# Twelve attention steps in another order on every engine, and value weights of 17 columns in 32-column groups

## The chip, the cores and the metric

The kernel runs on one core of a Trainium2 chip. The time is the device time of one execution in microseconds (us); the figure quoted is the median of several executions. TensorE is called PE (its weight loads PEld), VectorE DVE, ScalarE ACT, GpSimd POOL, and SyncE, which only issues DMAs here, SP.

## What is computed

A patch step (a product and a layer norm), one attention block and one mixture-of-experts block over 32 sequences of 188 tokens, 256 wide. The change touches attention alone. The reference, cut to it:

```python
q = x @ W_q; k = x @ W_k; v = x @ W_v
latent_kv = (k + v) @ W_down_kv
k_rec = (latent_kv @ W_up_k)   # 16 heads of 16
v_rec = (latent_kv @ W_up_v)
scores = einsum('bhqd,bhkd->bhqk', qh, k_rec) / sqrt(256)
scores = scores * decay          # exp(-0.01 |i - j|)
attn = softmax(scores)
out = einsum('bhqk,bhkd->bhqd', attn, v_rec) @ W_o
h = h + out
```

## The kernel before

Every engine runs its own program, and semaphores tie them together. Stages follow one another: patch step, attention, shared experts with the choice of tokens, experts. Attention takes one sequence ("batch" b) per turn, and each engine walks through `batch(b, par)` with twelve steps n = 0 to 11 (`NS`). A step handles two of the 24 score tiles of a batch, and what the engines do in a step belongs to different batches, since the stages are pipelined.

On PE a step n is: `take_max` (adds the negated row maximum to score tile n-1 by a product with a selection matrix), `scores` (of a tile 18 steps ahead, only to find row maxima), then in steps 1, 4, 7, 10 `weigh` (attention weights times values for four heads), a `job` that hangs on n, and `turned_scores` (the tile of step n+1, the one that is exponentiated). The jobs before are: n=0 second half of the value product (`project_values(b+1, ., 1)`), n=3 the q product (`project`), n=5 the k product, n=8 the output product (`project_out`), n=9 `turn_max` (three transposes of the row maxima), n=11 the first half of the value product of b+2 and `turn_x` (four transposes of the normed input of b+4).

On DVE a step is `row_max` (two tiles) and `times_decay` (one pair of tiles in PSUM), and further `invert` after n=5, `add_out` after n=9, `row_stats` after n=10, the row moments around n=11, and last `low_max`, which writes the low half of the turned maxima. `turn_x` in step 11 and `take_max` of the next batch wait for `low_max` (semaphore `mt_ready`), because the maxima and the turned input share a PSUM bank.

ACT does `exponential` in each step, brings products out of PSUM (`evacuate`, `keep_heads`, `evacuate_values`), makes high fp16 halves (`high`) and spreads values into the tiles V (`values`). POOL makes the low halves (`low`), sends the weighed heads out (`heads_out`), reads them back in dense form (`dense_heads`) and divides (`divide`). The q product in step 3 waits for `xtl_ready`, the low half of x that POOL makes with `low(XTL, ...)`.

`weigh` before takes 128 rows of V by 64 columns: two heads stand side by side in 32-column groups of their own, with zeros where a row belongs to the other head, and the two halves of PE's columns work on two head pairs.

```python
for t in range(3):
    for u in range(2):
        v = (t * HP + 2 * g + u) * 64
        last = mm(OB[64 * u:64 * u + 64, :], V[cpar][:, v:v + 64], PT[:, p:p + S], start=t == 0, stop=t == 2)
```

A product of float32 operands shows in the trace as two matmul records. The order of the work is written out by hand: the place of each call in `batch` is its place in the engine's queue. Lines in the profile before: L1455 take_max, L1441 scores, L1467 turned_scores, L1483 weigh, L1493 q and k product, L1504 values, L1516 output, L1529 turn_max, L1524 turn_x; L1127 row_max, L1136 times_decay, L1099 add_out, L1105 row_stats, L1112 and L1118 moments, L1083 low_max; L756 all copies of ACT, L805 exponential; L612 low, L618 and L619 heads_out, L628 dense_heads, L635 and L639 divide.

## Time and profile before

| what | value |
|---|---|
| median of 3 executions | 2015.07 us (2008.25 to 2016.47) |
| profiled execution | 2018.32 us, span of its instructions 2016.4 us |
| attention, from its first weighing record to the last | 192.0 to 928.8 us |
| batches in attention | 32 |

The profile shows one execution. The granted clock of PE is 1.0 at 2.4 GHz and 0.5 at 1.2 GHz. "Idle before" of a row is the time that the engine stood still ahead of it, with what ended it. Busy time of PE counts a matmul until its modelled end, so that a busy PE need not be one at its peak: the distance between starts tells what a matmul takes.

### The profile page before, as it was taken

The page shows a single profiled execution, that of the slowest core. Times are in us where ns is not written, and L with a number is a line of the kernel's source. Part 1 is how long each engine was busy: PE and PEld are TensorE (multiplying, and loading weights), DVE is VectorE, ACT ScalarE, POOL GpSimd, SP SyncE. Part 2 cuts the span into 40 slices and gives each one's busy share as a digit, 9 for nine tenths or more (in the row PEclk, how much of TensorE's full clock was granted, in tenths as well). Part 3 has the DMA queues.
Part 4 walks back from the last instruction along what each step waited for, and adds up shares of the span by engine and source line. Part 5 has one row for each costly group of instructions (what it writes and reads, how often), then busy time and mean ns, then how long its engine had stood idle before and what let it go on. Part 6 is the DMA issues. An engine that isn't in the chain of part 4 may idle for free.

```text
span 2016.4 us, 46453 instructions
## 1 busy us (share of the span) xinstructions
PE 1751.3 (87%) x14894; PEld 1327.7 (66%) x14894; DVE 1232.4 (61%) x3822; ACT 934.9 (46%) x2157; POOL 947.8 (47%) x945
## 2 busy tenths in 40 slices
PE   6857887887888878785899995999999999999997
PEld 5855665665666666563677773777777777777775
DVE  3884666666666666674767866555555555555551
ACT  3535555444554545452533254444444444444442
POOL 3852333333332333324622323466666666666665
PEclk9987888889987988898999996999999999999999
DMA  5524444444443434442321104243443344443322
GB/s 179 187 77 88 102 103 98 97 93 93 97 98 88 101 93 98 100 96 68 105 51 32 30 27 159 84 114 98 102 109 94 101 111 97 99 97 98 94 31 29
DMA packets 220234, 187.39 MB, mean 93 GB/s; under 512 B 165624, under 2 KB 200952, under 8 KB 214008
## 3 DMA queue, kind: packets, MB, share of 16 engines
q1 hardware_dynamic: 193272, 141.99, 26.0%
q0 software_dynamic: 26880, 44.36, 11.0%
q8 instruction: 46, 0.75, 0.2%
q14 instruction: 36, 0.29, 0.1%
HBM read 135.37 MB, written 50.44 MB: 92 GB/s over the span
## 4 chain that ended last, share of the span: by engine, by line
PE 70%; DVE 10%; issue 8%; POOL 6%; ACT 3%; DMA 2%; DVEq 1%; SPq 1%; POOLq 0%; ACTq 0%
PE psum L1742 24%; PE psum L1759 12%; PE psum L1483 6%; PE psum L1607 6%; PE psum L1493 4%; PE psum L1627 4%; PE psum L1467 2%; PE psum L1516 2%; PE psum L1455 2%; DVE psum L1136 2%; ACT arena L756 2%; PE psum L1504 2%; PE psum L1441 2%; POOL arena L612 1%; DVE arena L1127 1%
## 5 line engine op out<-in xcount | busy, mean ns | idle before, releaser
L1742 PE MATMUL psum<-arena,hidden 128*128 128x376 f16 x3072 | 493.7, 323 | 1.1 <-DVE arena L1362 0.9
L655 POOL TENSOR_TENSOR arena<-arena 128x376 f16<-128x376 f32 x320 | 319.7, 1001 | 353.7 <-ACT arena L756 352.3
L1742 PEld LDWEIGHTS psum<-arena,hidden 128*128 128x128 f16 x3072 | 301.1, 98 | 189.5 <-issue 1.9
L1136 DVE TENSOR_TENSOR psum<-psum,constants 128x376 f32<-128x376 f32 x384 | 212.9, 555 | 218.7 <-PE psum L1467 218.5
L756 ACT ACTIVATE arena<-arena 128x376 f16<-128x376 f32 (+5 forms) x610 | 283.6, 473 | 58.8 <-DVE arena L1298 46.6
L805 ACT ACTIVATE arena<-psum 128x376 f32<-128x376 f32 x384 | 184.9, 482 | 232.5 <-PE psum L1455 227.0
L971 ACT ACTIVATE arena<-psum 128x376 f32<-128x376 f32 x256 | 123.9, 484 | 342.7 <-PE psum L1742 342.7
L756 ACT ACTIVATE arena<-psum 128x376 f32<-128x376 f32 (+7 forms) x457 | 167.6, 398 | 228.5 <-PE psum L1483 123.5
L1127 DVE CUSTOM_DVE_ANT_0 arena<-psum,constants 128x188 f32<-128x188 f32 x768 | 237.6, 347 | 41.2 <-PE psum L1441 36.0
L1372 DVE SCALAR_TENSOR_TENSOR arena<-psum,arena 128x376 f32<-128x376 f32 x256 | 140.8, 550 | 189.9 <-ACT arena L971 188.5
L1759 PE MATMUL psum<-hidden,arena 128*128 128x256 f16 (+1 forms) x2304 | 256.6, 273 | 0.0
L1759 PEld LDWEIGHTS psum<-hidden,arena 128*128 128x128 f16 (+1 forms) x2304 | 229.8, 103 | 21.8
L1354 DVE SCALAR_TENSOR_TENSOR hidden<-arena,hidden 128x512 f16<-128x512 f32 x192 | 205.6, 1075 | 9.1 <-ACT hidden L756 9.1
L612 POOL TENSOR_TENSOR arena<-arena 128x376 f16<-128x376 f32 x128 | 115.2, 900 | 182.9 <-ACT arena L756 177.6
L701 POOL DMA_INDIRECT out<-hidden,arena x96 | 149.9, 1561 | 45.2 <-DVE hidden L1382 23.1
L1483 PE MATMUL psum<-arena 128*64 128x188 f32 x1536 | 167.6, 358 | 1.8 <-ACT arena L805 1.8
L1493 PE MATMUL psum<-arena,weights_hi 128*128 128x188 f16 x512 | 89.1, 276 | 74.7 <-POOL arena L612 65.0
L1455 PE MATMUL psum<-arena 128*128 128x188 f16 x768 | 135.5, 260 | 18.9 <-DVE psum L1136 18.6
L1382 DVE TENSOR_SCALAR hidden<-psum,arena 128x256 f32<-128x256 f32 x96 | 46.3, 482 | 164.7 <-PE psum L1759 164.5
L1441 PE MATMUL psum<-arena 96*128 96x188 f16 x768 | 136.2, 262 | 3.6 <-DVE arena L1127 2.6
L1607 PE MATMUL psum<-arena,weights_hi 128*128 128x376 f16 x512 | 136.3, 327 | 1.2 <-DVE arena L1165 1.2
L1467 PE MATMUL psum<-arena 96*128 96x188 f16 x768 | 135.1, 260 | 0.1
(158 smaller groups left out, 2801.2 us busy)
## 6 DMA issues: line engine op xcount, KB each, us to landing
arena<-q_halves SPq DMA_DIRECT2D x384, 47.0 KB, 2.1
arena<-k_halves SPq DMA_DIRECT2D x384, 47.0 KB, 2.1
arena<-e_g SPq DMA_DIRECT2D x16, 1024.0 KB
arena<-e_u SPq DMA_DIRECT2D x16, 1024.0 KB, 5.1
arena<-e_d SPq DMA_DIRECT2D x16, 1024.0 KB
arena<-x_t SPq DMA_DIRECT2D x32, 376.0 KB, 3.5
weighed<-arena POOLq DMA_DIRECT2D x32, 376.0 KB, 3.3
q_halves<-arena SPq DMA_DIRECT2D x32, 188.0 KB, 3.1
```

What stands on the lines that cost most here:

```text
L655: nc.gpsimd.tensor_tensor(dst, f, hi, ALU.subtract).then_inc(ready, 1)
L756: return nc.scalar.activation(dst, src, ACT.Copy, scale=scale)
L805: nc.scalar.activation(PT[:, i % 6 * 2 * S:(i % 6 + 1) * 2 * S], TB[i % 3], ACT.Exp).then_inc(exp_done, 1)
L1127: last = nc.vector.tensor_tensor_reduce(out=SC[i % 2 * 2 + u], in0=SB[i % 2][:, u * S:(u + 1) * S], in1=C[:, C_DECAY + t * S:C_DECAY + (t ...
L1136: nc.vector.tensor_tensor(TB[i % 3], TB[i % 3], C[:, at:at + 2 * S], ALU.mult).then_inc(multiplied, 1)
L1354: nc.vector.scalar_tensor_tensor(WEL[par][:, c], WST[:, c], WSCALE, WEH[par][:, c], ALU.mult, ALU.subtract).then_inc(wl_ready[i], 1)
L1441: last = mm(SB[i % 2][:, u * S:(u + 1) * S], block_tile(QD[cpar][0:2 * KR, :], a, t), KX[cpar][0:2 * KR, a * S:(a + 1) * S], start=True, s ...
L1455: last = mm(TB[i % 3][:, u * S:(u + 1) * S], block_tile(SEL, a, t), MT[cpar][:, 0:S], start=False, stop=True, skip_group_check=True)
L1483: last = mm(OB[64 * u:64 * u + 64, :], V[cpar][:, v:v + 64], PT[:, p:p + S], start=t == 0, stop=t == 2)
L1607: last = mm(bank[2 * (m % 2) + i][:, 0:CHUNK], w_, a, start=n == 0, stop=n == 5)
L1742: last = mm(bank[2 * (s % 2) + i][:, 0:CHUNK], w_, a, start=n == 0, stop=n == 5)
L1759: last = mm(bank[down_bank[m]][0:rows, 0:D], a, w_, start=n == 0, stop=n == 23)
```

## The change

1. `weigh` loads 17 value columns (16 and the row-sum column) per head into a 32-column group. Four heads go to the four column groups of PE. Per group of four heads there are four products of 128 rows, and then four of 64 rows (the middle tile, whose upper 64 rows belong to one head of a pair and whose lower ones to the other). Before there were six products of 128 rows and 64 columns. V shrinks from 64 to 32 columns for a pair.
2. The order of work changes in `batch` of all engines. PE: `turn_max` goes from n=9 to n=7, the first half of the values from n=11 to n=9 (and into a place of its own, the upper half of PSUM bank 5). ACT: `keep_heads` goes behind the copies of its step, `high_max` from n=10 to 8, x_norm from 8 to 9, the value copies are spread over n=2 and n=11. DVE: `low_max` from n=11 to 9, `add_out` from 9 to 10, `row_stats` from 10 to 11, the moments into the next batch. POOL: `low(XTL)` comes first, and `divide` goes from the end of a batch to the next one.
3. The columns of W_q and W_k are put in the order (half, d, pair), so that the reads of the dense q and k tiles are two DMAs of whole rows instead of six of 188-element pieces. SP reads KD before it waits for the inverse sums.
4. Two more batches are written out ahead of the loop, and one more behind it.

```diff
-        OB, XB, WB = bank[5][:, 0:S], bank[6], bank[7]
+        OB, VB, XB, WB = bank[5][:, 0:S], bank[5][:, D:2 * D], bank[6], bank[7]
...
-            for b in range(-4, 2):
+            for b in range(-4, 4):
                 body(b, b % 2)
-            with nc.Fori(1, B // 2 - 2, engines=bass.OrderedEngineSet([eng.engine]), head_slot={eng.engine: 0}) as i:
+            with nc.Fori(2, B // 2 - 2, engines=bass.OrderedEngineSet([eng.engine]), head_slot={eng.engine: 0}) as i:
                 body(2 * i, 0)
                 body(2 * i + 1, 1)
-            for b in range(B - 4, B + 2):
+            for b in range(B - 4, B + 3):
...
-            def read(blocks, dense, dram, c, lows, par, landed):
-                for h2 in range(2):
-                    for r in range(3):
-                        p = h2 * KR + r * HD
-                        if blocks is not None:
-                            dst = blocks[par][p:p + HD, :].rearrange("p (a n) -> p a n", n=CW)[:, :, h2 * HS:h2 * HS + S]
-                        else:
-                            dst = dense[par][p:p + HD, :].rearrange("p (a n) -> p a n", n=S)
-                        sp.dma_start(dst, rows(dram, c, h2, lows[r])).then_inc(landed[par], 16)
+            def read(blocks, dense, dram, c, single, par, landed):
+                both = 1 - single // 2
+                if blocks is None:
+                    for low, r, n in ((1, single, 1), (0, both, 2)):
+                        src = dram[c, low, :, :, :].rearrange("h (d a) n -> (h d) (a n)", a=HP)
+                        sp.dma_start(dense[par][32 * r:32 * (r + n), :], src.unsqueeze(0).broadcast_to((n, 32, HP * S)) if n > 1 else src).then_inc(landed[par], 16)
+                else:
+                    for h2 in range(2):
+                        for r in range(3):
+                            p = 32 * r + HD * h2
+                            sp.dma_start(blocks[par][p:p + HD, :].rearrange("p (a n) -> p a n", n=CW)[:, :, h2 * HS:h2 * HS + S],
+                                         dram[c, int(r == single), h2, :, :].rearrange("(d a) n -> d a n", a=HP)).then_inc(landed[par], 16)
...
-                    read(QD, None, q_dram, c, (0, 1, 0), par, s_in)
+                    read(QD, None, q_dram, c, 0, par, s_in)
                     sp.wait_ge(k_out, 16 * c + 16)
                     hold(sp)
-                    read(None, KX, k_dram, c, (0, 0, 1), par, s_in)
+                    read(None, KX, k_dram, c, 2, par, s_in)
                 if valid(b + 1):
                     at_least(sp, st_done, NS * b)
                     hold(sp)
-                    read(None, QX, q_dram, b + 1, (0, 1, 0), 1 - par, st_in)
+                    read(None, QX, q_dram, b + 1, 0, 1 - par, st_in)
+                    read(KD, None, k_dram, b + 1, 2, 1 - par, st_in)
                 c = b - 1
                 if valid(c):
                     sp.wait_ge(sums_inverse, c + 1)
                     hold(sp)
+                    at_least(sp, rd_in, 64 * c)
+                    hold(sp)
                     sp.dma_start(r_dram[:, :].rearrange("h (q n) -> (h q) n", q=4), RS[0:64, :]).then_inc(rs_out, 16)
-                if valid(b + 1):
-                    read(KD, None, k_dram, b + 1, (0, 0, 1), 1 - par, st_in)
...
             def batch(b, par):
+                low(XTL[1 - par], XF, XTH[1 - par], xth_ready, b + 3, xtl_ready)
+                heads_out(b - 1, 1 - par)
+                divide(b - 2)
                 low(OTL, ON, OTH, oth_ready, b - 2, otl_ready)
-                heads_out(b - 1, 1 - par)
-                low(XTL[1 - par], XF, XTH[1 - par], xth_ready, b + 3, xtl_ready)
+                low(QS[:, 2 * S:4 * S], QF, QS[:, 0:2 * S], qh_ready, b + 3, ql_ready)
                 dense_heads(b - 1)
-                low(QS[:, 2 * S:4 * S], QF, QS[:, 0:2 * S], qh_ready, b + 3, ql_ready)
                 low(KS2[:, 2 * S:4 * S], KF, KS2[:, 0:2 * S], kh_ready, b + 3, kl_ready)
-                divide(b - 1)
...
             def batch(b, par):
                 for n in range(NS):
                     exponential(b, par, n)
-                    if n == 1:
-                        keep_heads(b - 1, 1 - par, 3)
-                    elif n % 3 == 1:
-                        keep_heads(b, par, (n - 4) // 3)
                     if n == 0:
                         evacuate(XF, XB, b + 3, xt_done, xf_ready)
                     elif n == 1:
                         if valid(b + 3) and valid(b + 1):
-                            act.wait_ge(v_done, b + 2)
+                            act.wait_ge(v_done, 2 * b + 4)
                         high(XTH[1 - par], XF, b + 3, xf_ready, xth_ready)
-                        evacuate_values(b + 1)
-                    elif n in (2, 3):
-                        values(b + 1, 1 - par, n - 2)
+                        keep_heads(b - 1, 1 - par, 3)
+                    elif n == 2:
+                        evacuate_values(b + 1, 1)
+                        values(b + 1, 1 - par, 0)
+                    elif n == 3:
+                        values(b + 1, 1 - par, 1)
                     elif n == 4:
                         evacuate(QF, WB, b + 3, q_done, qf_ready)
+                        keep_heads(b, par, 0)
                     elif n == 5:
                         high(QS[:, 0:2 * S], QF, b + 3, qf_ready, qh_ready, q_out)
                     elif n == 6:
                         evacuate(KF, WB, b + 3, k_done, kf_ready)
                     elif n == 7:
                         high(KS2[:, 0:2 * S], KF, b + 3, kf_ready, kh_ready, k_out)
+                        keep_heads(b, par, 1)
                     elif n == 8:
+                        high_max(b + 1, 1 - par)
+                    elif n == 9:
                         x_norm(b + 4)
                     elif n == 10:
-                        high_max(b + 1, 1 - par)
+                        keep_heads(b, par, 2)
+                    elif n == 11:
+                        evacuate_values(b + 2, 0)
...
             def batch(b, par):
                 for n in range(NS):
-                    if n == 11:
-                        row_moments(b - 2)
+                    if n == 0:
+                        row_moments(b - 3)
                     row_max(b, par, n)
                     times_decay(b, n)
-                    if n == 5:
+                    if n == 0:
+                        keep_moments(b - 3)
+                    elif n == 5:
                         invert(b - 1)
                     elif n == 9:
+                        low_max(b + 1, 1 - par)
+                    elif n == 10:
                         add_out(b - 2)
-                    elif n == 10:
+                    elif n == 11:
                         row_stats(b - 2, 0)
                         row_stats(b - 2, 1)
-                    elif n == 11:
-                        keep_moments(b - 2)
-                        low_max(b + 1, 1 - par)
...
                 at_least(pe, os_ready, 4 * c + g)
+                if g == 3 and valid(c + 2):
+                    pe.wait_ge(vf_ready, 2 * c + 5)
                 pe.wait_ge(exp_done, NS * c + 3 * g + 3)
-                for t in range(3):
-                    for u in range(2):
-                        v = (t * HP + 2 * g + u) * 64
-                        p = (6 * g + 3 * u + t) % NS * S
-                        last = mm(OB[64 * u:64 * u + 64, :], V[cpar][:, v:v + 64], PT[:, p:p + S], start=t == 0, stop=t == 2)
+                for n in range(2):
+                    for k in range(4):
+                        a, h2 = 2 * g + k // 2, k % 2
+                        t, p0, rows = ((0, 0, 128), (2, 0, 128))[h2] if n == 0 else (1, 64 * h2, 64)
+                        v, p = (t * HP + a) * 32, (3 * a + t) % NS * S
+                        last = mm(OB[32 * k:32 * k + HD + 1, :], V[cpar][p0:p0 + rows, v:v + HD + 1], PT[p0:p0 + rows, p:p + S],
+                                  start=n == 0, stop=n == 1)
                 last.then_inc(weighed, 1)
...
                 if n == 0 and valid(b + 1):
+                    if valid(b - 3):
+                        pe.wait_ge(y_added, b - 2)
+                    else:
+                        pe.wait_ge(kf_ready, b + 3 if valid(b + 2) else B)
                     project_values(b + 1, 1 - par, 1)
                 if n == 3 and valid(b + 3):
                     if valid(b + 1):
-                        pe.wait_ge(vf_ready, b + 2)
+                        pe.wait_ge(vf_ready, 2 * b + 4)
                     else:
                         at_least(pe, kf_ready, b + 3)
                     pe.wait_ge(xtl_ready, b + 4)
...
                 if n == 5 and valid(b + 3):
                     pe.wait_ge(qf_ready, b + 4)
                     project(b + 3, 1 - par, W_K, k_done)
+                if n == 7 and valid(b + 1):
+                    if isinstance(b, int) and b + 1 == 0:
+                        pe.wait_ge(cleared, 3)
+                    if valid(b + 3):
+                        pe.wait_ge(xf_ready, b + 4)
+                    pe.wait_ge(scaled, NS * b + 2 * NS)
+                    turn_max(b + 1, 1 - par)
                 if n == 8 and valid(b - 2):
                     if valid(b + 3):
                         pe.wait_ge(kf_ready, b + 4)
                     elif valid(b + 1):
-                        pe.wait_ge(vf_ready, b + 2)
+                        pe.wait_ge(vf_ready, 2 * b + 4)
                     else:
-                        pe.wait_ge(y_added, b - 2)
+                        at_least(pe, y_added, b - 2)
                     pe.wait_ge(otl_ready, b - 1)
                     project_out(b - 2)
-                if n == 9 and valid(b + 1):
-                    if isinstance(b, int) and b + 1 == 0:
-                        pe.wait_ge(cleared, 2)
-                    if valid(b + 3):
-                        pe.wait_ge(xf_ready, b + 4)
-                    pe.wait_ge(scaled, NS * b + 2 * NS)
-                    turn_max(b + 1, 1 - par)
-                if n == 11 and valid(b + 2):
+                if n == 9 and valid(b + 2):
                     pe.wait_ge(xtl_ready, b + 3)
-                    if valid(b - 2):
-                        pe.wait_ge(y_added, b - 1)
-                    else:
-                        pe.wait_ge(kf_ready, b + 4)
+                    if valid(b + 1):
+                        pe.wait_ge(vf_ready, 2 * b + 4)
+                    if valid(b):
+                        pe.wait_ge(os_ready, 4 * b + 2)
                     project_values(b + 2, par, 0)
...
+    by_pair = np.arange(D).reshape(HP, 2, HD).transpose(1, 2, 0).reshape(D)
```

POOL's order, one batch of the loop before (low halves of the output input, `heads_out`, low half of x, `dense_heads`, low halves of q and k, `divide`):

```order
L612 TENSOR_TENSOR arena<-arena 128x376
L616 ISA
L618 DMA arena<-arena 64x1x47
L619 DMA weighed<-arena 128x4x188
L611 REGISTER_ALU
L612 TENSOR_TENSOR arena<-arena 128x376
L623 ISA
L628 DMA arena<-weighed 128x1x188 x2
L612 TENSOR_TENSOR arena<-arena 128x376 x2
L635 TENSOR_TENSOR arena<-arena 128x376
L639 CAST arena<-arena 128x376
```

The same batch on POOL in the changed kernel, where the first row is the low half of x:

```order
L613 TENSOR_TENSOR arena<-arena 128x376
L617 ISA
L621 DMA arena<-arena 64x1x47
L622 DMA weighed<-arena 128x4x188
L635 ISA
L638 TENSOR_TENSOR arena<-arena 128x376
L642 CAST arena<-arena 128x376
L613 TENSOR_TENSOR arena<-arena 128x376 x2
L626 ISA
L631 DMA arena<-weighed 128x1x188 x2
L613 TENSOR_TENSOR arena<-arena 128x376
```

The low half of x no longer stands behind the two DMAs of `heads_out`, and `divide` (L638, L642) of the batch before stands in the middle.

DVE's order before, from `times_decay` of step 10 on: statistics, moments, step 11, and `low_max` (8x192) at its end:

```order
L1136 TENSOR_TENSOR psum<-psum,constants 128x376
L1105 BN_STATS arena<-hidden 94x6
L1105 ISA
L1105 BN_STATS arena<-hidden 94x6
L1112 BN_AGGR arena<-arena 94x2 x2
L1127 ISA arena<-psum,constants 128x188
L1136 TENSOR_TENSOR psum<-psum,constants 128x376
L1118 COPY mean_var<-arena 94x4
L1083 SCALAR_TENSOR_TENSOR arena<-psum,arena 8x192 x2
```

In the changed kernel, from `times_decay` of step 9 on:

```order
L1143 TENSOR_TENSOR psum<-psum,constants 128x376
L1087 ISA
L1090 SCALAR_TENSOR_TENSOR arena<-psum,arena 8x192 x2
L1130 REGISTER_ALU
L1134 ISA arena<-psum,constants 128x188
L1143 TENSOR_TENSOR psum<-psum,constants 128x376
L1106 ISA
L1106 SCALAR_TENSOR_TENSOR hidden<-psum,hidden 94x512
```

`low_max` now stands behind step 9 and ahead of `add_out` and the statistics.

PE's order before around a weighing (step 4, then the turned scores and the next step):

```order
L1441 MATMUL psum<-arena 128x188 x2
L1476 ISA
L1483 MATMUL psum<-arena 64x188 x6
L1467 MATMUL psum<-arena 128x188 x2
L1455 MATMUL psum<-arena 128x188 x2
```

And in the changed kernel (the first number of a product is its weight columns):

```order
L1450 MATMUL psum<-arena 128x188 x2
L1485 ISA
L1495 MATMUL psum<-arena 17x188 x8
L1476 MATMUL psum<-arena 128x188 x2
L1464 MATMUL psum<-arena 128x188 x2
```

Six products of 64 columns became eight of 17; nothing else around them moved.

## Rows read from the trace of the kernel before

**Rows 1.** The page's busy time, share of the span and instructions of each engine.
```profile
PE 1751.3 (87%) x14894; PEld 1327.7 (66%) x14894; DVE 1232.4 (61%) x3822; ACT 934.9 (46%) x2157; POOL 947.8 (47%) x945
```
**Rows 2.** PE's waits, 150 to 935 us: waiter, releaser: total us, times, longest.
```profile
PE psum L1493 <- POOL arena L612: 65.0, 31, 3.3
PE psum L1524 <- DVE arena L1083: 54.4, 29, 2.7
PE psum L1455 <- DVE psum L1136: 18.6, 80, 0.8
```
**Rows 3.** Line L618 (`heads_out`), 300 to 800 us: first and last start, landing.
```profile
L618 POOL DMA_DIRECT2D arena<-arena x21: 627/627/641, 302.5 to 791.3; - x21
...
DMA to landing us min/median/max: 1.9/2.1/2.5
```
**Rows 4.** Timeline of PE: start, length, line, shapes (weights, moving).
```profile
311.04 1.18 PE L1483 MATMUL psum<-arena 128*64 128x188 f32 x12
312.15 0.34 PE L1467 MATMUL psum<-arena 96*128 96x188 f16 x2
312.32 0.33 PE L1455 MATMUL psum<-arena 128*128 128x188 f16 x2
...
316.98 0.38 PE L1504 MATMUL psum<-weights_hi,arena 128*128 128x256 f16 x2
...
317.31 0.38 PE L1504 MATMUL psum<-weights_hi,arena 128*128 128x256 f16 x2
...
319.65 0.51 PE L1524 MATMUL psum<-constants,arena 94*128 94x94 f32 x4 [1.86 <-DVE arena L1083]
320.00 0.33 PE L1467 MATMUL psum<-arena 96*128 96x188 f16 x2
```
**Rows 5.** Timeline of DVE from step 9 to step 11 of a batch.
```profile
339.59 0.68 DVE L1099 SCALAR_TENSOR_TENSOR hidden<-psum,hidden 94x512 f32 x1
340.19 0.34 DVE L1127 CUSTOM_DVE_ANT_0 arena<-psum,constants 128x188 f32<-128x188 f32 x1
...
340.73 0.55 DVE L1136 TENSOR_TENSOR psum<-psum,constants 128x376 f32<-128x376 f32 x1
341.19 0.74 DVE L1105 BATCH_NORM_STATS2 arena<-hidden 94x6 f32 x2
342.08 0.24 DVE L1112 BATCH_NORM_AGGREGATE arena<-arena 94x2 f32<-94x6 f32 x2
...
343.40 0.16 DVE L1118 COPY mean_var<-arena 94x4 f32 x1
343.59 0.71 DVE L1083 SCALAR_TENSOR_TENSOR arena<-psum,arena 8x192 f16<-8x192 f32 x2
```
**Rows 6.** Timeline of PE: router products in four 32-column groups, then full width.
```profile
970.20 0.34 PE L1638 MATMUL psum<-arena,weights_hi 128*32 128x376 f16 x4
...
971.01 0.33 PE L1638 MATMUL psum<-arena,weights_hi 128*32 128x376 f16 x4
971.28 0.33 PE L1607 MATMUL psum<-arena,weights_hi 128*128 128x376 f16 x1
```
**Rows 7.** Timeline of POOL: `heads_out` and the low half of x.
```profile
325.98 0.63 POOL L618 DMA_DIRECT2D arena<-arena  x1 [4.68 <-ACT arena L756]
...
327.44 0.91 POOL L612 TENSOR_TENSOR arena<-arena 128x376 f16<-128x376 f32 x1
```
**Rows 8.** Timeline of ACT: `keep_heads`, then the high half of x.
```profile
325.03 0.33 ACT L756 ACTIVATE arena<-psum 128x188 f32<-128x188 f32 x1 [1.47 <-PE psum L1483]
325.25 0.51 ACT L756 ACTIVATE arena<-arena 128x376 f16<-128x376 f32 x1
```
**Rows 9.** Windows: us, then busy (count) of PE, PEld, DVE, ACT, POOL; PEclk; DMA share; GB/s.
```profile
50.00:100.00 50.00, 43.77 (x379) 41.91 (x377) 42.86 (x170) 26.23 (x53) 39.64 (x22) 0.97 0.58 188
...
150.00:188.00 38.00, 24.66 (x160) 17.45 (x161) 13.10 (x82) 17.05 (x37) 8.08 (x9) 0.64 0.36 77
...
300.00:400.00 100.00, 80.09 (x725) 61.27 (x724) 66.84 (x291) 52.36 (x142) 32.68 (x43) 0.89 0.42 97
```

More of the change, by code:

```diff
@@ L189, in build @@
         MT = [at2(HS, F16) for _ in range(2)]
-        V = [at2(3 * HP * 64) for _ in range(2)]
+        V = [at2(3 * HP * 32) for _ in range(2)]
         at3 = Place()
@@ L829, in x_norm, with evacuate_values @@
                 last.then_inc(xn_ready, 1)
-            def evacuate_values(c):
+            def evacuate_values(c, t):
                 if valid(c):
-                    act.wait_ge(v_done, c + 1)
-                    copy(VF[:, 0:D], WB[:, 0:D], 1.0 / WSCALE)
-                    copy(VF[0:TAIL, D:2 * D], WB[0:TAIL, D:2 * D], 1.0 / WSCALE).then_inc(vf_ready, 1)
+                    act.wait_ge(v_done, 2 * c + t + 1)
+                    if t == 0:
+                        at_least(act, v_ready, 5 * c)
+                        copy(VF[:, 0:D], VB, 1.0 / WSCALE).then_inc(vf_ready, 1)
+                    else:
+                        copy(VF[0:TAIL, D:2 * D], WB[0:TAIL, D:2 * D], 1.0 / WSCALE).then_inc(vf_ready, 1)
             def values(c, par, h2):
@@ L844, in values @@
                     at_least(act, weighed, 4 * c - 4)
-                to = V[par].rearrange("p (t a h w) -> p t a h w", t=3, a=HP, h=2)[:, :, :, h2, 0:HD]
-                first, second = (VF[:, w * D:(w + 1) * D].rearrange("p (a h d) -> p a h d", h=2, d=HD)[:, :, h2, :] for w in range(2))
-                if h2 == 0:
-                    copy(to[:, 0], first).then_inc(v_ready, 1)
-                    copy(to[0:TAIL, 1], second[0:TAIL]).then_inc(v_ready, 1)
-                else:
-                    copy(to[64:128, 1], first[0:64]).then_inc(v_ready, 1)
-                    copy(to[0:64, 2], first[64:128]).then_inc(v_ready, 1)
-                    copy(to[64:64 + TAIL, 2], second[0:TAIL]).then_inc(v_ready, 1)
+                for t, p0, n, q0, at in (((0, 0, 128, 0, 0), (1, 0, TAIL, 0, D)), ((1, 64, 64, 0, 0), (2, 0, 64, 64, 0), (2, 64, TAIL, 0, D)))[h2]:
+                    src = VF[q0:q0 + n, at:at + D].rearrange("p (a h d) -> p a h d", h=2, d=HD)[:, :, h2, :]
+                    dst = V[par][p0:p0 + n, :].rearrange("p (t a w) -> p t a w", t=3, w=32)[:, t, :, 0:HD]
+                    copy(dst, src).then_inc(v_ready, 1)
             def high_max(c, par):
@@ L1497, in project_values @@
             def project_values(c, par, t):
-                rows = (128, TAIL)[t]
+                rows, to = ((128, VB), (TAIL, WB[0:TAIL, D:2 * D]))[t]
                 n = 0
@@ L1503, in project_values @@
                     for a, w_ in split3(XTH[par][:, x], XTL[par][:, x], WH[:, w], WL[:, w]):
-                        last = mm(WB[0:rows, t * D:(t + 1) * D], a, w_, start=n == 0, stop=n == 5)
+                        last = mm(to, a, w_, start=n == 0, stop=n == 5)
                         n += 1
-                if t == 1:
-                    last.then_inc(v_done, 1)
+                last.then_inc(v_done, 1)
             def project_out(c):
@@ L1534, in job @@
                 if n == 0 and valid(b + 1):
+                    if valid(b - 3):
+                        pe.wait_ge(y_added, b - 2)
+                    else:
+                        pe.wait_ge(kf_ready, b + 3 if valid(b + 2) else B)
                     project_values(b + 1, 1 - par, 1)
@@ L1795, in score_tables @@
     select = (p[:, None, None] % 32 == np.arange(HP)[None, :, None]) & (p[:, None, None] // 32 % 2 == row // HS) & inside
-    value_rows = np.zeros((128, 3, HP, 2, 32), np.float32)
-    for h2 in range(2):
-        value_rows[:, :, :, h2, HD] = (inside & (row // HS == h2)).reshape(3, 128).T[:, :, None]
+    value_rows = np.zeros((128, 3, HP, 32), np.float32)
+    value_rows[:, :, :, HD] = inside.reshape(3, 128).T[:, :, None]
     return {"select": (16.0 * select).astype(np.float16).reshape(128, HP * CW), "blank": np.zeros((128, HP * CW), np.float16),
-            "value_rows": value_rows.reshape(128, 3 * HP * 64)}
+            "value_rows": value_rows.reshape(128, 3 * HP * 32)}
 def kernel(x, L0_tok_conv_w, L0_tok_conv_b, L0_tok_ln_gamma, L0_tok_ln_beta, L0_attn_W_q, L0_attn_W_k, L0_attn_W_v,
```

17 lines of the change are left out of this document (9 added, 8 removed).

## The prediction

> **What bounds the kernel now.** The page comes first: PE is the busiest engine at 87% of the span and nothing else passes 61% [rows 1], so the question is where PE stands still inside the changed stage. The table of PE's waits over attention answers it [rows 2]. Two rows carry nearly all: the q product waits for POOL's low half of x, 65.0 us in 31 waits, which is 2.1 us per batch; and `turn_x` waits for DVE's `low_max`, 54.4 us in 29 waits, 1.9 us per batch. A third row, `take_max` waiting for `times_decay`, is 18.6 us or 0.6 us per batch; that is the lockstep between PE and DVE. The length of a batch comes from one POOL line that occurs once in each: 21 starts from 302.5 to 791.3 us are 20 batches of 24.44 us [rows 3]. Last the windows: in a steady stretch of 100 us PE is busy 80.09 us at a granted clock of 0.89 [rows 9], so that about 22% of the time runs at the lower level of 1.2 GHz.
>
> Both waits have a cause that the timelines show. POOL waits 4.68 us for ACT before the first DMA of `heads_out`, issues for 1.46 us (325.98 to 327.44), and only then makes the low half of x in 0.91 us [rows 7], although ACT had finished the high half at 325.76 [rows 8]. DVE comes to `low_max` at 343.59, behind `add_out`, the statistics, the moments and the two steps 10 and 11 [rows 5].
>
> **The change, part by part.** The account is per batch, in the profiled execution (2018.32 us), 24.44 us before.
>
> *The wait for the low half of x.* In the new order POOL makes it first. Counted from PE's start s of step 1: `take_max` takes 0.17 us (312.15 to 312.32 for such a pair) [rows 4], the exponential some 0.5 us and the high half 0.51 us [rows 8], with 0.2 us of latency that is s + 1.3; POOL's 0.91 us [rows 7] make it s + 2.25. PE meanwhile has step 1 (three pairs and a weighing, 1.4 us), step 2 (0.5 us) and two pairs of step 3 (0.34 us), so it asks at s + 2.25. I take the 2.1 us as gone; a rest of 0 to 0.3 us is in the range. `keep_heads` now follows the high half, which delays `heads_out` to about s + 2.3. Its sums land 0.63 + 2.1 us after the issue begins at the latest [rows 3, 7], that is s + 5.0, and DVE wants them after step 5, at about s + 5.9. This cover is thin: 0.9 us.
>
> *The wait for `low_max`.* `turn_max` at step 7 is asked for only after `row_max` of step 6, which `take_max` of step 7 has waited for anyway. `low_max` then stands behind step 9 on DVE, and `turn_x` behind weighing and two steps of PE later. The 1.9 us go as a wait for this row. ACT's copy of q now stands ahead of `keep_heads`, which helps step 5, and a copy of values stands behind the exponential of step 2, which may hurt step 3; I let the two cancel.
>
> *The weighing.* Now 1.11 us from its first start to the next line's (311.04 to 312.15) for 12 records in two halves of the columns [rows 4]. Six pairs at 188 columns and two cycles per column are 6 x 0.157 = 0.94 us, and 0.17 us go before the full width resumes. The nearest row for four column groups is the router product: 24 matmuls in six rounds of four, the sixth round 0.81 us after the first, 0.162 us per round, and 0.27 us from the last round to the next line [rows 6]. Each of its matmuls is as long as a record here (376 columns at one cycle). Eight products are 16 records or four rounds: 4 x 0.157 + 0.17 = 0.80 us, plus something where the second four products, of 64 rows, begin. The rows show 0.10 us more at a change of width than inside one (0.27 against 0.17) and I take 0.05 to 0.1, so 0.85 us, a gain of 0.26 us each and 1.04 us per batch. The bounds: 0.31 us each if the change of rows costs nothing, and no gain if the 64-row products with different rows follow one another (four rounds for them instead of two, 0.31 us more).
>
> The Trainium skill ("TensorEngine Tiling (Array Packing)", Key Properties) says that changing the tiling mode drains the engine, and by that each group now pays one drain more, between 128-row and 64-row tiles. No row here shows that one. By the difference seen at a change of width it is the 0.1 us already in the sum; were it as large as the 0.27 us of the router, a weighing would gain 0.1 us instead of 0.26, and the sum below would be 20.4 us per batch and 1892 us.
>
> *What takes their place.* With both waits gone DVE becomes the partner that PE waits for. A DVE step is 0.54 us of `row_max` (340.19 to 340.73) and 0.46 us of `times_decay` (340.73 to 341.19), 1.00 us [rows 5]. From step 9 to step 0 it does four such steps, `low_max` 0.71, `add_out` 0.60, statistics 0.89, moments 0.24 and 0.16: 6.6 us. PE does in its steps 9, 10, 11 and 0: four times three pairs (2.0), two halves of the value product at 0.66 (316.98 to 317.31 is three of six), one weighing (0.9 with its entry) and `turn_x` 0.35: 4.6 us [rows 4, 5]. PE therefore comes about 2.0 us too early, less some 0.3 us that DVE is ahead after PE's long step 8, so 1.7 us, in steps 0 and 1. The short steps 2 and 6 (0.5 us on PE) cost 0.3 us each as they do now. Sum of waits for DVE: 2.3 us against the present 0.6, 1.7 us more. Everything else DVE, ACT and POOL do is the same work in another place. SP issues 16 reads per batch instead of 24; PE waits for none of them in [rows 2], so they count as nothing. The written-out batches and the extra one at the end are 1 us at most.
>
> *The clock.* At 0.89 about 5.4 us of each batch run at 1.2 GHz, and with PE busy four fifths of it that loses 2.15 us. Of the windows, PE 88% busy has 0.97 (50 to 100 us), 80% has 0.89, 65% has 0.64 [rows 9]. After the change PE's busy share is higher, and no single pause is as long as the 1.86 us seen ahead of `turn_x` [rows 4]. I take 0.95, a loss of 0.85 us: 1.3 us come back. The bounds are nothing and 2.15 us.
>
> *Sum.* 24.44 - 2.1 - 1.9 - 1.04 + 1.7 - 1.3 = 19.8 us per batch, 4.6 us less. With 31 batches between the first and the last that is 143 us. The filling and the emptying of the pipeline keep their latencies. 2018 - 143 = 1875 us for the profiled execution, and the median of the runs stands 3 us below it: **1872 us**.
>
> **The rivals.**
>
> *A. More is gained than that.* DVE waits are smaller because PE's jobs hide them, and the clock is fully granted: 24.44 - 2.1 - 1.9 - 1.24 + 1.2 - 2.15 = 18.25 us, 6.2 less, 1823 us. For it speaks that DVE's work of a batch, 12 steps and 3 us, is only 15 us; against it that this work is bunched in four steps.
>
> *B. Only part arrives.* The weighing gets no shorter, the clock stays at 0.89, and 0.6 us of a wait for POOL or ACT remain: 24.44 - 4.0 + 0.6 + 1.4 = 22.4 us, 2.0 less, 1953 us. With the clock alone unchanged it is 21.1 us, 1912 us. For it speaks that the low half of x and PE meet at the same s + 2.25; against it that less weighing takes less PE work out of the way of DVE, so that not all of the loss counts.
>
> *C. The sums come late.* DVE stands in step 5 for `invert`, because `heads_out` is now behind `keep_heads` and the low half. Its margin is 0.9 us; if the DMA's landing stretched from 2.1 to 4 us, each batch would lose 1 us: 20.8 us, 1903 us. Landings here stay within 1.9 to 2.5 us [rows 3].
>
> *D. Slower.* The pauses before DVE are shorter but more, spread over steps 0, 1, 3 and 7, and the clock answers by staying at its lower level. PE's own work, 24.44 less 4.6 of waits and 2.15 of clock is 17.7, less 1.04 is 16.6 us; at half the clock that is 33 us, 8.8 more per batch, 2290 us. It decides once PE's 16.6 us and about 1 us of waits have grown to 24.44: by 6.8 us, or 0.41 of the work, which at half the clock then fills 13.7 of 24.44 us, a mean granted clock of 0.72. The window of 150 to 188 us does have 0.64, but with PE busy 65% [rows 9].
>
> *E. The change does nothing measurable.* It would need the waits to reappear elsewhere in full, 4 us per batch; no engine has that much work in one place.
>
> **How the numbers follow.** The forecast has 0.55 (1835 to 1905), A 0.12, B with its clock half 0.22, C 0.05, D 0.03, E 0.03. The likeliest time is 1872 us. The range must leave out at most 0.2: it reaches down to A and up to most of B, 1822 to 1945 us. A measurement of this kernel tells 0.5% (10 us) from no change. Faster by more than that: 0.94; the same: 0.02; slower: 0.04.
>
> **What would show it.** In the profile after, the row of the q product waiting for POOL should be below 15 us in total, the row of `turn_x` waiting for `low_max` absent, and the rows of PE waiting for `times_decay` grown from 18.6 to 50 to 80 us. The line of `heads_out` should recur every 19.8 us (18.3 to 21.5). A weighing should take 0.80 to 0.9 us to the next line's start. The granted clock between 300 and 700 us should be 0.92 to 1.0. The prediction is wrong if POOL still releases the q product for over 1 us per batch, if DVE waits for a DMA in step 5, or if the clock falls below 0.85.

## The result: 1.5% slower, and the profile after

The changed kernel takes 2042.69 us (median of 4 executions, 2039.16 to 2046.86) against 2013.17 us for the kernel before (also four executions); the ratio is 1.0149 (95% interval 1.0119 to 1.0179). The forecast was 1872 us, with a chance of 0.94 on faster. The profiled execution has a span of 2037.0 us.

The page of the changed kernel, its busy line, the hardware queue that SP issues on, and the engines' shares of the chain that ended last:

```profile
PE 1729.7 (85%) x15406; PEld 1262.4 (62%) x15406; DVE 1217.6 (60%) x3823; ACT 943.9 (46%) x2157; POOL 949.4 (47%) x945
...
q1 hardware_dynamic: 145272, 141.18, 24.4%
...
PE 52%; issue 19%; DMA 15%; POOL 7%; DVE 4%; SPq 2%; ACT 2%; POOLq 0%; DVEq 0%; ACTq 0%
```

PE is busy a little less than in [rows 1], and DMAs now make up 15% of the chain, against 2% before. PE's waits between 150 and 960 us:

```profile
PE psum L1450 <- DMA arena<-k_halves: 108.0, 29, 8.0
PE psum L1464 <- DVE psum L1143: 67.1, 117, 1.5
...
PE psum L1506 <- POOL arena L613: 4.5, 3, 2.2
```

The two large waits of [rows 2] are gone as forecast: the q product (now L1506) waits for POOL 4.5 us in all, and no row is left of `turn_x` waiting for `low_max`. In their place the score products (L1450) wait 108.0 us for k and q tiles. DVE has a wait of its own in the same stretch:

```profile
DVE arena L1099 <- DMA arena<-arena: 98.9, 25, 5.0
```

L1099 is `invert` in step 5; it waits for the sums that `heads_out` sends. The line of that DMA, 300 to 800 us, against [rows 3]:

```profile
L621 POOL DMA_DIRECT2D arena<-arena x20: 627/627/641, 318.2 to 778.1; - x20
...
DMA to landing us min/median/max: 2.0/7.4/8.0
```

The landing went from 2.1 to 7.4 us. Its data are 11.8 KB both times, and it is issued by POOL, whose DMAs keep their form. The larger DMA of `heads_out`, the heads themselves, is late too; it landed in 3.3 us before and is now the largest DMA of the chain (9% of the span), and POOL waits for it 92.3 us in 19 waits (300 to 800 us) before `dense_heads` and, behind that, the low half of k:

```profile
weighed<-arena POOLq DMA_DIRECT2D x32, 376.0 KB, 8.5
```

What lies ahead of both shows in SP's queue (start, length of the issuing):

```profile
414.00 1.16 SPq L470 DMA_DIRECT2D arena<-k_halves  x2
415.35 1.16 SPq L470 DMA_DIRECT2D arena<-q_halves  x2
416.62 5.38 SPq L475 DMA_DIRECT2D arena<-k_halves  x6
```

and on POOL and DVE in the same batch:

```profile
415.96 0.63 POOL L621 DMA_DIRECT2D arena<-arena  x1 [0.26 <-issue]
```

DVE, start and length of `invert`, and in brackets its idle time before it:

```profile
423.30 0.44 DVE L1099 RECIPROCAL arena<-arena 64x47 f32<-64x47 f32 x1 [3.87 <-DMA arena<-arena]
```

The four dense reads (L470) go out between 414.0 and 416.5 us, the sums are issued at 415.96, and DVE gets them at 423.30, after 3.87 us of standing still. PE resumes at 423.58, after 3.13 us of waiting for the tiles. One of the two DMAs of each L470 pair carries 188 KB with a leading repeat of 2.

The lateness eats the whole gain of the steady stretch: 20 starts of `heads_out` from 318.2 to 778.1 us are 24.2 us per batch, against 24.44 before. The time gets longer mainly at the start of attention: the first `heads_out` stands at 220.5 us instead of 207.7, and the last of the 32 at 950.7 instead of 930.2.

### The profile page after: what moved, and what is told of

It is laid out like the page before. It is cut to its first block, busy times and chain, and to the rows that moved or that the text cites. A ratio compares the mean times of both kernels' runs of the same rounds, so it can differ in the third digit from the quotient of the medians.

```text
span 2037.0 us, 47015 instructions
## 1 busy us (share of the span) xinstructions
PE 1729.7 (85%) x15406; PEld 1262.4 (62%) x15406; DVE 1217.6 (60%) x3823; ACT 943.9 (46%) x2157; POOL 949.4 (47%) x945
## 4 chain that ended last, share of the span: by engine, by line
PE 52%; issue 19%; DMA 15%; POOL 7%; DVE 4%; SPq 2%; ACT 2%; POOLq 0%; DVEq 0%; ACTq 0%
PE psum L1758 24%; PE psum L1775 12%; DMA weighed<-arena 9%; PE psum L1623 6%; PE psum L1643 4%; POOL arena L613 2%; DMA arena<-k_halves 2%; POOL hidden L591 1%; POOL arena L596 1%; DMA arena<-arena 1%; SPq L475 1%; PE psum L1738 1%; POOL arena L631 1%; DMA inverse_sums<-arena 1%; ACT arena L759 1%
## 5 line engine op out<-in xcount | busy, mean ns | idle before, releaser
L759 ACT ACTIVATE arena<-psum 128x188 f32<-128x188 f32 (+7 forms) x457 | 175.5, 398 | 162.3 <-PE psum L1738 57.9
L1450 PE MATMUL psum<-arena 96*128 96x188 f16 x768 | 141.7, 272 | 120.8 <-DMA arena<-k_halves 108.0
L1450 PEld LDWEIGHTS psum<-arena 96*128 96x128 f16 x768 | 74.4, 107 | 131.4 <-issue 80.3
L1495 PE MATMUL psum<-arena 128*17 128x188 f32 (+1 forms) x2048 | 141.5, 370 | 0.8 <-ACT arena L808 0.7
L1476 PE MATMUL psum<-arena 96*128 96x188 f16 x768 | 138.1, 264 | 0.0
```

The source lines that it names most:

```text
L759: return nc.scalar.activation(dst, src, ACT.Copy, scale=scale)
L1450: last = mm(SB[i % 2][:, u * S:(u + 1) * S], block_tile(QD[cpar][0:2 * KR, :], a, t), KX[cpar][0:2 * KR, a * S:(a + 1) * S], start=True, s ...
```

## The experiments

Theory P: a read whose pattern begins with a repeat of 2 is spread over two DMA engines only, drains slowly, and everything that has a part on those two engines lands late. Theory Q: the reads' new place in SP's order is at fault. The runs are compared with runs of the kernel before on the same chip (2010 to 2014 us there).

**e1, two plain reads in place of the repeated one.**

```diff
-                    for low, r, n in ((1, single, 1), (0, both, 2)):
+                    for low, r in ((1, single), (0, both), (0, both + 1)):
...
+                        sp.dma_start(dense[par][32 * r:32 * (r + 1), :], src).then_inc(landed[par], 16)
```

> The changed kernel, but the read that puts the same k or q rows into two groups of 32 partitions (a leading repeat of 2 in the source, 64 packets of 3008 bytes) is made as two DMAs of 32 rows each. Theory P (the repeat of 2 leads the pattern, so the DMA is spread over few engines, drains slowly and holds up others behind it): the sums land 2 to 3 us after their issue as before instead of 7.4, DVE no longer waits for them in step 5, PE's wait for the k tile (108 us) is under 10 us, and the time is 1860 to 1900 us. Theory Q (the trouble is where the reads now stand in SP's order, ahead of the inverse sums and beside the heads going out): the landing of the sums stays over 5 us and the time over 2000 us.

Measured: 1848.81 us, ratio to before 0.9178 (0.9163 to 0.9194). The same bytes in the same order, and 194 us less than the changed kernel. The line of `heads_out` in e1, from 300 to 700 us:

```profile
L621 POOL DMA_DIRECT2D arena<-arena x22: 624/627/641, 317.2 to 696.1; - x22
...
DMA to landing us min/median/max: 2.1/2.4/2.6
```

The window of 300 to 700 us, the changed kernel first and e1 below (columns as in [rows 9]):

```profile
300.00:700.00 400.00, 304.88 (x3137) 209.96 (x3137) 255.65 (x1127) 205.38 (x539) 125.00 (x161) 0.86 0.39 96
```

and e1:

```profile
300.00:700.00 400.00, 357.00 (x4236) 253.16 (x4235) 344.76 (x1526) 278.40 (x733) 172.41 (x223) 1.00 0.52 131
```

21 batches take 378.9 us, 18.04 us each. PE's waits from 150 to 960 us:

```profile
PE psum L1464 <- DVE psum L1143: 50.9, 113, 1.3
...
PE psum L1450 <- DMA arena<-k_halves: 16.1, 20, 1.8
```

and the heads' own DMA in e1:

```profile
weighed<-arena POOLq DMA_DIRECT2D x32, 376.0 KB, 4.2
```

The landing is what P said, and Q as the cause of the whole loss falls. Two things missed what P expected: the time is 11 us below its range, and PE still waits 16.1 us for the tiles where under 10 were expected.

How many engines the repeated read uses can be counted from the packets of queue q1 on the pages:

```profile
q1 hardware_dynamic: 147192, 141.19, 26.7%
```

e1 has 1920 packets more than the changed kernel, 60 for each of 32 batches. The data packets are equal (64 rows of 3008 bytes, whether in one DMA or two), so the 60 are completions: four plain DMAs against two repeated ones. A plain one has 16 (e4 below has 46080 more than e1, 1440 a batch: 1344 are data, since 12 DMAs of 128 pieces replace 192 rows, and 96 are the completions of six more DMAs). So 64 - 60 = 4 completions fall to two repeated DMAs, 2 each. e7 below confirms it with one repeated DMA left: 960 more than the changed kernel, 30 a batch, which is 32 - 2. The Trainium skill ("DMA: Bandwidth & Descriptors", Rules for kernel authors) says just this: a leading zero-stride broadcast of c copies confines the whole DMA to at most c engines. The count agrees with it.

The kept trace also has the start and length of every packet, and there both halves of P can be seen. First the slow drain: in the changed kernel's batch shown above, the 192 packets of 3008 bytes of the four dense reads take from 415.1 to 427.7 us, and from 417 us on 1.8 of them are in flight in the mean, never more than three. In e1's batch (L470 at 407.8 and 409.5 us) the same 192 take from 408.8 to 412.4 us, 8.9 in flight in the mean. Second the late landings of others: the sums' DMA closes with 16 packets of 4 bytes. In the changed kernel 14 of them start between 417.3 and 417.6 us and the other two at 422.5 and 422.6. The heads' DMA behind it has 14 closing packets at 419.2 to 419.5 us and two at 424.1 and 424.2. In e1 all 16 of the sums start between 408.4 and 408.9 us. Two shares of sixteen are late, and DVE starts `invert` at 423.30 us, 0.7 us after the later of the two. It is so in most batches: of the 16, exactly 14 start within 2.4 us of the issue in 24 of the changed kernel's 32 batches and in 29 of e3's 32, and all 16 do in every batch of e1 and of the kernel before.

**e2, the read of KD back behind the inverse sums** (the repeat kept).

```diff
-                    read(KD, None, k_dram, b + 1, 2, 1 - par, st_in)
...
+                if valid(b + 1):
+                    read(KD, None, k_dram, b + 1, 2, 1 - par, st_in)
```

> The changed kernel, with the read of KD moved back behind the write of the inverse sums, as before; the reads with the leading repeat stay. Theory P: the repeated reads stay ahead of the heads on the same few engines, so the sums still land late, 5 us or more, and the time is 2000 to 2060 us. Theory Q: the sums land in 2 to 3 us and the time falls to 1860 to 1920 us.

Measured: 2003.38 us, ratio 0.9935 (0.9916 to 0.9954). The sums still land late; the landing of `heads_out` in e2, 300 to 700 us:

```profile
DMA to landing us min/median/max: 2.2/5.9/6.9
```

This is inside P's range. Moving the one read of KD removes 39 of the 194 us, so with the repeats in place its position matters; with plain reads the old place was not run.

**e3, only the new reads in the kernel before.**

```diff
-                        sp.dma_start(dst, rows(dram, c, h2, lows[r])).then_inc(landed[par], 16)
...
+                    for low, r, n in ((1, single, 1), (0, both, 2)):
+                        src = dram[c, low, :, :, :].rearrange("h (d a) n -> (h d) (a n)", a=HP)
+                        sp.dma_start(dense[par][32 * r:32 * (r + n), :], src.unsqueeze(0).broadcast_to((n, 32, HP * S)) if n > 1 else src).then_inc(landed[par], 16)
```

> The kernel before with its own orders and weighing, and only the new reads (column order of the q and k weights, dense tiles in one DMA of 32 rows and one of 64 with the leading repeat of 2). Theory P: the 64-row reads land 5 us or more after their issue and PE comes to wait for k tiles or DVE for sums: 2030 to 2150 us. Theory Q, and a third, that fewer DMAs help or cost nothing in any order: 2000 to 2020 us.

Measured: 2035.25 us, ratio 1.0102 (1.0081 to 1.0122). Three executions lie between 2034.33 and 2035.88 us; a fourth took 4392.33 us, for a cause that is not known. The result is in P's range. The landing is slow here too, but DVE waits for the sums only 0.5 us in all between 300 and 700 us, and PE for the tiles 14.7 us in attention. The landing of `heads_out` in e3:

```profile
DMA to landing us min/median/max: 4.9/5.7/6.3
```

So the new reads cost 21 us under the old orders. Under the new ones they cost 191 us (against e4 below), and the repeat alone 194 us (against e1).

**e4, the reads of before in the changed kernel** (`read`, its waits and the order of the weights' columns as before).

```diff
-                    for low, r, n in ((1, single, 1), (0, both, 2)):
...
+            def rows(dram, c, h2, low):
+                return dram[c, low, :, :, :].rearrange("c (a h d) n -> h d (c a) n", h=2, d=HD)[h2]
...
+                        sp.dma_start(dst, rows(dram, c, h2, lows[r])).then_inc(landed[par], 16)
```

> The changed kernel with the reads of before (six DMAs of 16 partitions for every tile, weights' columns in their own order), all orders and the weighing of 17 columns kept. Theory P: 1860 to 1910 us, since the reads alone are at fault; SP's issue time rises back by about 3.6 us per batch, which may cost up to 20 us beside e1. Theory Q: over 2000 us.

Measured: 1851.83 us, ratio 0.9194 (0.9179 to 0.9210). 24 small reads cost 3 us more than the 18 of e1. The time is 8 us below P's range. Without the repeat the new layout of q and k brings these 3 us and no more.

**e5, the orders alone** (e4 with V of 64 columns and six products per weighing).

```diff
-                        last = mm(OB[32 * k:32 * k + HD + 1, :], V[cpar][p0:p0 + rows, v:v + HD + 1], PT[p0:p0 + rows, p:p + S],
...
+                        last = mm(OB[64 * u:64 * u + 64, :], V[cpar][:, v:v + 64], PT[:, p:p + S], start=t == 0, stop=t == 2)
```

> The reads and the weighing of before (six products of 64 columns) under the new orders: the orders alone. The working of the prediction gives them 24.44 - 2.1 - 1.9 + 1.4 - 1.3 = 20.5 us per batch; corrected by what e4 showed (18.0 us per batch instead of 19.8, and a clock of 1.00), and with four weighings longer by 0.22 us each of which about half lies under DVE's work: 18.5 us per batch, 1860 to 1875 us. A rival, that the shorter weighing was the larger part: 1900 us or more.

Measured: 1866.98 us, ratio 0.9280 (0.9251 to 0.9310). The orders carry 143 us of the 165 that e1 gains.

**e6, the weighing alone** (before with the eight products of 17 columns and the narrow V).

```diff
-                        last = mm(OB[64 * u:64 * u + 64, :], V[cpar][:, v:v + 64], PT[:, p:p + S], start=t == 0, stop=t == 2)
...
+                        last = mm(OB[32 * k:32 * k + HD + 1, :], V[cpar][p0:p0 + rows, v:v + HD + 1], PT[p0:p0 + rows, p:p + S],
```

> The kernel before with only the weighing changed (eight products of 17 columns, narrow V). PE sits in front of both waits either way, and a shorter weighing makes heads and the low half of x begin earlier, so the gain reaches the end: 4 x 0.22 us per batch or a little less, 1985 to 2000 us. A rival, that it is hidden by the waits or eaten by a clock that falls as PE is busy less: 2005 to 2020 us.

Measured: 1998.16 us (1984.49 to 2005.89), ratio 0.9935 (0.9904 to 0.9966). The weighing brings 12 us here and 15 under the new orders (e4 against e5). The executions of e6 scatter by 21 us, so that the 12 is good to about 6 either way.

**e7, the repeat in one tile, QX.**

```diff
+                    if repeat:
+                        src = dram[c, 0, :, :, :].rearrange("h (d a) n -> (h d) (a n)", a=HP)
+                        sp.dma_start(dense[par][32 * both:32 * (both + 2), :], src.unsqueeze(0).broadcast_to((2, 32, HP * S))).then_inc(landed[par], 16)
...
-                    read(None, QX, q_dram, b + 1, 0, 1 - par, st_in)
+                    read(None, QX, q_dram, b + 1, 0, 1 - par, st_in, True)
```

> The kernel e1 with the leading repeat of 2 put back in one of the two tiles, QX alone, and the tiles of k in single DMAs. If the slow drain of each such DMA is the cause, half of it comes back: the sums land in 4 to 6 us, and since their margin ahead of step 5 is about 2 us in e1, DVE waits 1 to 2 us per batch: 1880 to 1950 us. If it is only the sum of two such DMAs in a row that passes a margin: 1850 to 1870 us. If it is all due to one of them already: over 2000 us.

Measured: 1919.17 us, ratio 0.9538 (0.9508 to 0.9568), in the range but not by the way expected. The sums land on time and DVE does not wait for them; PE waits for tiles instead. The landing of `heads_out` in e7:

```profile
DMA to landing us min/median/max: 2.0/2.3/2.9
```

and PE's wait for the tiles in e7, 150 to 960 us:

```profile
PE psum L1453 <- DMA arena<-k_halves: 53.9, 27, 5.4
```

The packets of q1 on e7's page, for the count under e1:

```profile
q1 hardware_dynamic: 146232, 141.19, 26.1%
```

One repeated read, the one of QX, is enough to make tiles late. It does not make the sums late: in e7 it is issued at 416.06 us, 5.3 us after the heads, while in the changed kernel the repeated read of KX goes out ahead of them. Whether KX's alone would make the sums late was not run. e7 also issues the repeated read first of its pair, where the changed kernel issues it second.

**e8, no change of rows inside a weighing** (the second four products take all 128 rows, so they add the other head's rows and the output differs), in e1.

```diff
-                        t, p0, rows = ((0, 0, 128), (2, 0, 128))[h2] if n == 0 else (1, 64 * h2, 64)
+                        t, p0, rows = ((0, 0, 128), (2, 0, 128))[h2] if n == 0 else (1, 0, 128)
```

> The kernel e1 with the second four products of a weighing over all 128 rows instead of the 64 of one head each (the middle tile then adds the other head's rows, so the output differs): no change of rows inside a weighing. If that change costs what is left over four rounds of 0.157 and 0.17 us, the weighing falls from 0.89 to 0.80 us and the time by 0 to 8 us. If the 64-row products gained something by running side by side in rows, it gets longer: 0.9 us or more. A third, that nothing changes: the 0.09 us belong to the narrow groups as such.

Measured: 1847.86 us, as e1. A weighing and the next line on PE's timeline, in e1:

```profile
404.87 0.95 PE L1495 MATMUL psum<-arena 128*17 128x188 f32 x16
405.76 0.33 PE L1476 MATMUL psum<-arena 96*128 96x188 f16 x2
```

and in e8:

```profile
403.58 0.83 PE L1495 MATMUL psum<-arena 128*17 128x188 f32 x16
404.35 0.34 PE L1476 MATMUL psum<-arena 96*128 96x188 f16 x2
```

0.89 us against 0.77; over all complete weighings between 300 and 700 us the medians are 0.885 and 0.764. The starts of the 16 records show where the 0.12 us lie. In e1 the four rounds of four start at 0, 0.17, 0.44 and 0.61 us, in e8 at 0, 0.17, 0.33 and 0.49 us: the step from 128 to 64 rows takes 0.27 us instead of 0.16. Four times 0.12 us per batch would be 15 us, and the time shows 1. Where they go is not shown: PE waits for `times_decay` 50.7 us in e8 as in e1 (50.9), and for the k tiles 21.3 instead of 16.1.

**e9, the heads ahead of the low half of x on POOL**, in e1.

```diff
-                low(XTL[1 - par], XF, XTH[1 - par], xth_ready, b + 3, xtl_ready)
                 heads_out(b - 1, 1 - par)
+                low(XTL[1 - par], XF, XTH[1 - par], xth_ready, b + 3, xtl_ready)
```

> The kernel e1 with POOL's two DMAs of the heads issued ahead of the low half of x, as before. By the prediction's account the low half is then ready 1.45 us plus the wait for keep_heads later than PE asks for it; PE's waits for POOL in step 3 come back at 1.5 to 2 us per batch, partly covered by the waits for DVE that they replace: 1870 to 1900 us. A rival, that the slack in e1 covers it: 1845 to 1855 us.

Measured: 1933.87 us, ratio 0.9591 (0.9550 to 0.9632): 85 us for one line's place, and 34 us above the expected range. The wait is back as it was, and the granted clock falls from 1.00 to 0.94. PE's waits in e9, 150 to 960 us:

```profile
PE psum L1506 <- POOL arena L613: 68.7, 31, 3.4
PE psum L1464 <- DVE psum L1143: 55.8, 131, 1.6
```

and its window of 300 to 700 us:

```profile
300.00:700.00 400.00, 325.67 (x3592) 229.19 (x3590) 295.50 (x1306) 238.20 (x624) 141.53 (x186) 0.94 0.45 110
```

**e10, `low_max` behind step 11 on DVE**, in e1.

```diff
-                    elif n == 9:
-                        low_max(b + 1, 1 - par)
...
+                        low_max(b + 1, 1 - par)
```

> The kernel e1 with low_max on DVE put back behind step 11 and the statistics, everything else of the new orders kept. PE waits again ahead of turn_x in step 11, and DVE's work is the same in sum, so most of the 1.9 us of before come back, less the waits of steps 0 and 1 that now fall into it: 1 to 1.5 us per batch, 1880 to 1895 us. A rival, that turn_max at step 7 was the part that mattered: 1845 to 1860 us.

Measured: 1874.12 us, ratio 0.9301 (0.9268 to 0.9334): 25 us more than e1, and 6 us below the expected range. The wait of `turn_x` returns, and the one for `times_decay` shrinks to what it was (PE's waits in e10, 150 to 960 us):

```profile
PE psum L1535 <- DVE arena L1090: 53.7, 29, 1.9
...
PE psum L1463 <- DVE psum L1143: 18.6, 74, 1.7
```

## Why the prediction was wrong

**The step that failed** is the sentence on SP under "What takes their place": "SP issues 16 reads per batch instead of 24; PE waits for none of them in [rows 2], so they count as nothing." Fewer reads were taken for no more burden. The term stood at nothing and measured 194 us (e1 against the changed kernel), 6.3 us per batch, seen as 108.0 us of PE waiting for tiles and 98.9 us of DVE waiting for sums. That no wait showed before said nothing of reads of another form: the trace had no row of a DMA with a leading repeat, and its cost should have been bounded. By the count under e1, the 64 packets of 3008 bytes run 32 on each of two engines, where 16 engines would have four each. The rule of the Trainium skill that is cited there was to be had beforehand, and I did not weigh it. Rival C named one of the victims, the sums and DVE's step 5, with a landing of 4 us and a chance of 0.05, and "DVE waits for a DMA in step 5" was among the signs of being wrong. The landing became 7.4 us, and the lateness of the tiles and of the heads was not thought of.

**Both old waits go**: right. 65.0 became 4.5 us, and 54.4 became nothing. e9 prices the first term at 85 us where 2.1 us per batch, 65 us, stood in the sum: the clock is part of it. e10 prices the second at 25 us where 1.9 us per batch, 59 us, stood. Most of that difference is the trade that the prediction charged as a term of its own, waits for `times_decay` taking the place: they go from 18.6 us in e10 to 50.9 us in e1.

**The weighing**: right in kind, a little over-sized. 0.89 us against the 0.85 taken, a gain of 0.22 instead of 0.26 us. Of 4 x 0.22 x 31 = 27 us, 12 to 15 arrive at the end (e5, e6). The extra for the change of rows was taken at 0.05 us and is 0.12 (e8). The prediction's other price for it, 0.27 us, was added up wrongly: 0.80 + 0.27 is 1.07 us, a gain of 0.04 us instead of 0.1, which makes 20.7 us per batch instead of 20.4.

**Waits for DVE**: 2.3 us per batch were taken, 50.9 / 31 = 1.6 us measured in e1, in the direction of rival A. **The clock**: 0.95 was taken; it is 0.86 in the changed kernel, where pauses of 3 us and more have come in, and 1.00 in e1. In e1, with pauses before DVE of at most 0.8 us in that stretch, it is not lowered, so the mechanism of rival D did not appear.

**The sum**, tried where the failed step is undone: 19.8 us per batch forecast, 18.04 measured. This is nearer to rival A's 18.25: the waits for DVE and the clock both came out better than the terms taken. Yet e1's 1849 us is only 23 us below the forecast 1872. The figures of the steady stretch do not hold for all 31 batches: from the first `heads_out` to the last, a batch takes 23.31 us before (207.7 to 930.2 us) and 17.85 us in e1 (205.7 to 759.2 us), 5.5 us less where the steady stretch has 6.4 less. Multiplying a steady figure by 31 was a second, smaller mistake, and that the forecast lies near e1 is in part luck: one error made the gain too small, the other too large.

**Why the new reads cost 21 us under the old orders and 191 under the new.** The margins of step 5 can be read from the traces. Before, `invert` starts 7.3 us after the issue of the sums at 325.98 us [rows 7] (6.0 us in the batches on either side), and a landing takes 2.1 us:

```profile
333.28 0.43 DVE L1092 RECIPROCAL arena<-arena 64x47 f32<-64x47 f32 x1
```

Under the new orders, in e1, it starts 3.5 us after the issue, and a landing takes 2.4 us:

```profile
407.00 0.63 POOL L621 DMA_DIRECT2D arena<-arena  x1 [0.24 <-issue]
```

and on DVE:

```profile
410.46 0.43 DVE L1099 RECIPROCAL arena<-arena 64x47 f32<-64x47 f32 x1
```

So the margin of 0.9 us that the prediction worked out was right (1.1 here), and it was 4 to 5 us before. A landing of 5.7 us (e3) still fits in 6.0 us, and one of 7.4 us does not fit in 3.5: in the batch shown DVE was free for `invert` at 419.43 us and stood still for 3.87 us. How the 191 us divide between late sums, late tiles and late heads is not shown, since they fall into the same stretch of a batch.

## What to carry to other kernels

When a DMA's form changes, look at the slowest dimension of its pattern before counting issues or bytes: a leading repeat of 2 put 188 KB on two of sixteen engines, and the victims were the tile itself and the DMAs of another queue. A reorder that removes waits also removes the slack that hid slow transfers, so price every transfer of the changed code against the new margins. And where a mixed change comes out slower, split it: here the form of one read separated 2043 us from 1849 us.

## What the runs showed that I had not expected

In e1 the granted clock was 1.00 from 300 to 700 us, where no wait of PE was longer than 1.3 us. With one pause of 1.9 us in each batch it was 0.95 (e10), and with one of 2.3 us in the mean 0.94 (e9). An 11.8 KB DMA from POOL landed 5 us later because of reads that SP had issued, and only two of its sixteen shares were late. The change of rows inside a weighing costs 0.12 us, and the time does not show it.
